# A two-layer graph network on one core: seven blocks split in rows 3 and 5, three masks and the low parts of x moved on VectorE

## The reference, cut to what matters

```python
# x: 4096 x 128, adj: 4096 x 4096 (nonnegative, mostly zero), all fp32
node = x @ W1                                   # 4096 x 16
hw   = einsum('nc,kcf->nkf', x, W2)             # 16 products of 128 x 128 weights
x0   = einsum('nk,nkf->nf', node, hw)
x1   = layernorm(x + relu(adj @ x0 + node @ b0))
msg  = x1 @ W + B
w    = where(adj < 1, exp(-(1/adj - 1)**2 * 2), 0)
out  = layernorm(x1 + w @ msg)
```

## Time and profile before

| what | value |
|---|---|
| median of 3 runs | 548.31 us (548.08 to 548.4) |
| the profiled execution, its own time | 548.46 us |
| its span | 546.6 us |
| PE busy | 541.2 us (99%), granted clock 1.0 throughout |
| DVE busy | 504.6 us (92%) |
| ACT busy | 498.2 us (91%) |
| POOL busy | 83.3 us (15%), all in stage one |
| DMA read | 139.62 MB |

### The profile page before, as it was taken

How to read it: one execution, slowest core, us unless ns; L and a number is a source line. 1 busy time by engine, 2 the same in 40 slices (tenths; PEclk the granted TensorE clock), 3 DMA queues, 4 the chain that set the end, 5 groups by cost and what they waited for, 6 DMA issues and landing times.

```text
span 546.6 us, 5236 instructions
## 1 busy us (share of the span) xinstructions
PE 541.2 (99%) x1800; PEld 332.0 (61%) x1800; DVE 504.6 (92%) x561; ACT 498.2 (91%) x449; POOL 83.3 (15%) x76
## 2 busy tenths in 40 slices
PE   9999999999999999999999999999999999999996
PEld 8888888655655565556555655565556556554444
DVE  5767777899999999999999999999999999999887
ACT  4778888669999999999999998999899899999994
POOL 1789989500000000000000000000000000000000
PEclk9999999999999999999999999999999999999999
DMA  5894000199998988888888898898988886870003
GB/s 165 321 424 173 27 2 0 31 367 422 414 360 300 339 335 315 303 330 314 334 306 314 321 349 305 312 317 320 327 315 308 316 330 236 322 267 1 0 19 135
DMA packets 23130, 142.05 MB, mean 260 GB/s; under 512 B 2720, under 2 KB 3264, under 8 KB 6720
## 3 DMA queue, kind: packets, MB, share of 16 engines
q1 hardware_dynamic: 22960, 141.46, 69.7%
q10 hardware_dynamic: 144, 0.26, 0.2%
HBM read 139.62 MB, written 2.10 MB: 259 GB/s over the span
## 4 chain that ended last, share of the span: by engine, by line
PE 99%; ACT 0%; DVE 0%; issue 0%; POOL 0%; ACTq 0%; POOLq 0%
PE kept_ps L526 20%; PE l_ps L526 18%; PE acc_ps L475 14%; PE acc_ps L464 7%; PE acc_ps L465 7%; PE acc_ps L466 7%; PE hw_ps L434 6%; PE hw_ps L440 5%; PE hw_ps L437 5%; PE acc_ps L526 2%; PE acc_ps L412 1%; PE var_ps L507 1%; PE acc_ps L481 1%; PE hw_ps L554 1%; PE acc_ps L536 0%; PE kept_ps L536 0%
## 5 line engine op out<-in xcount | busy, mean ns | idle before, releaser
L935 DVE SCALAR_TENSOR_TENSOR wt_pair<-wt_pair 128x2048 f32<-128x2048 f32 x60 | 136.9, 2283 | 1.3 <-DMA wt_pair<-adjT_dram 1.3
L642 ACT ACTIVATE wt_pair<-wt_pair 128x4096 f32<-128x4096 f32 (+1 forms) x33 | 108.9, 3300 | 11.7 <-DVE wt_pair L935 11.7
L647 ACT ACTIVATE wt_pair<-wt_pair 128x4096 f32<-128x4096 f32 (+1 forms) x33 | 109.1, 3307 | 0.5
L526 PE MATMUL kept_ps<-wt_pair,msg 128*128 128x512 f32 x240 | 107.9, 592 | 0.0
L923 DVE TENSOR_TENSOR row_lo<-rows,adj_hi 128x2048 fp32r<-128x2048 f32 x42 | 96.3, 2292 | 1.4
L526 PE MATMUL l_ps<-wt_pair,msg 128*128 128x512 f32 x216 | 97.1, 592 | 0.0
L626 ACT ACTIVATE prods<-hw_ps,node 128x128 f32<-128x128 f32 x256 | 73.1, 373 | 19.1 <-PE hw_ps L440 17.5
L890 DVE SCALAR_TENSOR_TENSOR part_acc<-hw_ps,node,part_acc 128x128 f32<-128x128 f32 x224 | 60.8, 343 | 20.7 <-PE hw_ps L440 20.7
L475 PE MATMUL acc_ps<-rows,x 128*128 128x512 f32 x176 | 78.8, 592 | 0.0
L464 PE MATMUL acc_ps<-adj_hi,x_hi 128*128 128x512 f32 x168 | 75.5, 449 | 0.0
L526 PEld LDWEIGHTS kept_ps<-wt_pair,msg 128*128 128x128 f32 x240 | 45.4, 190 | 49.3 <-issue 47.8
(11 more groups left out here) (122 smaller groups left out, 603.4 us busy)
## 6 DMA issues: line engine op xcount, KB each, us to landing
rows<-adjT_dram SPq DMA_DIRECT2D x68, 1024.0 KB, 4.9
wt_pair<-adjT_dram SPq DMA_DIRECT2D x60, 1024.0 KB, 4.8
x_in<-xT_dram SPq DMA_DIRECT2D x8, 256.0 KB, 3.6
x_row<-xT_dram SPq DMA_DIRECT2D x8, 256.0 KB, 5.1
outT_dram<-sumT SPq DMA_DIRECT2D x7, 256.0 KB, 2.0
W_in<-W_dram SPq DMA_DIRECT2D x3, 256.0 KB, 4.8
W_in<-W_dram ACTq DMA_DIRECT2D x1, 256.0 KB, 3.7
outT_dram<-sumT SPq DMA_DIRECT2D x2, 128.0 KB, 1.9
```

Of the source, the lines that this page charges most:

```text
L526: mm = pe.matmul(out, msg[:, c % 2, k, :], wt[t][:, k, :], start=(first and k == 0), stop=(last and k == CH - 1))
L642: act.activation(w, w, ACT.Ln, bias=TINY).then_inc(ln_made, 1)
L647: act.activation(w, w, ACT.Exp, scale=-1.0).then_inc(inv_made, 1)
L935: dve.scalar_tensor_tensor(out=w, in0=w, scalar=1.0, in1=w, op0=ALU.is_lt, op1=ALU.mult).then_inc(made, 1)
```

## The change

- The split blocks are a table by row. Rows 0, 2, 4 and 6 stay; row 1 gains block 6 (tile 14), row 3 block 2 (tile 26), row 5 block 2 (tile 42), row 7 block 6 (tile 62): 46 tiles are split.
- Block 2 of x0 needs high and low parts, one `round_x0` and one `remainder_of_x0` more. The low parts of blocks 1, 4 and 6 now overwrite x0 (with a wait for the last tile of that block that isn't split); only block 2 has memory of its own for its low part.
- The squares of pairs 28 and 44 go from DVE to ACT.
- Masks 0, 1 and 2 are done in stage one on DVE, after the sums of blocks 2, 4 and 6. For this SP loads the first six column tiles ahead of the first five row tiles.
- The low part of x of the next block is made on DVE, in the middle of `sum_over_k`, no longer on POOL.
- The written orders on DVE and ACT are changed all along stage two.

```diff
+SPLIT_IN_ROW = ((3, 5, 7), (1, 3, 5, 6, 7), (1, 3, 4, 5, 6, 7), (1, 2, 3, 4, 5, 6, 7), (1, 3, 4, 5, 6, 7), (1, 2, 3, 4, 5, 6, 7), (1, 3, 4, 5, 6, 7), (1, 3, 4, 5, 6, 7))
+LO_APART = tuple(g for g in SPLIT if any(g in row and g not in SPLIT_IN_ROW[-1] for row in SPLIT_IN_ROW))
+MORE_ON_ACT = (28, 44)
+MASKS_AFTER = (2, 4, 6)
...
-            return (m - FIRST_PAIR) % 4 >= 2 or m >= BY_TILE
+            return ((m - FIRST_PAIR) % 4 >= 2 and m not in MORE_ON_ACT) or m >= BY_TILE
...
+            for t in range(WT_RING - LATE_SLOTS):
+                load_wt(t)
             for i in range(ROW_RING):
                 load_row_tile(i)
-            for t in range(WT_RING - LATE_SLOTS):
-                load_wt(t)
...
                 for q in range(QUARTERS):
+                    if q == QUARTERS // 2 and g + 1 < NB:
+                        remainder_of_x(g + 1)
                     dve.wait_ge(hw_made[0], g * GROUPS + 2 * q + 2)
...
+                if g in MASKS_AFTER:
+                    mask(MASKS_AFTER.index(g))
...
             for g in range(NB):
-                if g + 1 < NB:
-                    remainder_of_x(g + 1)
                 fold(g)
```

More of the change, by code:

```diff
@@ L730, in _ @@
             take_ln(10)
+            square(1)
             take_inverse(10)
+            take_exp(8)
+            take_square(10)
+            take_ln(12)
             log_variance(1)
-            take_square(10)
+            take_inverse(12)
             inverse_root(1)
-            take_exp(8)
-            take_ln(12)
             take_exp(10)
-            take_inverse(12)
             take_ln(14)
+            take_exp(12)
             take_inverse(14)
-            take_exp(12)
             take_square(14)
@@ L910, in remainder_of_x0 @@
                 dve.wait_ge(x0_hi_made, n + 1)
+                if g not in LO_APART:
+                    at_least(dve, row_tile_done, max([i + 1 for i in range(g, TILES, NB) if not is_split(i)], default=0))
                 dve.tensor_tensor(x0_lo[g], x0[:, whole, :], x0_hi[:, mine, :],
@@ L1189, in _ @@
             mask(36)
+            split_row_tile(43)
             round_square(4)
+            take_square(32)
+            remainder_of_square(4)
             split_row_tile(44)
-            remainder_of_square(4)
-            take_square(32)
             mask(37)
+            split_row_tile(45)
+            scale_row(4)
             add_part(29)
+            split_row_tile(46)
             mask(38)
-            split_row_tile(45)
+            copy_messages(4)
+            add_part(31)
             mask(39)
-            scale_row(4)
-            split_row_tile(46)
-            add_part(31)
-            copy_messages(4)
-            mask(40)
             split_row_tile(47)
@@ L1254, in _ @@
             scale_row(6)
+            split_row_tile(62)
+            add_part(47)
+            copy_messages(6)
+            mask(56)
             split_row_tile(63)
-            copy_messages(6)
-            add_part(47)
-            mask(56)
             take_square(52)
@@ L1261, in _ @@
             take_square(54)
-            mask(58)
+            add_part(49)
             take_square(55)
@@ L1265, in _ @@
             mask(60)
+            mask(58)
+            mask(61)
             mask(59)
+            scale_row(7)
             take_square(56)
-            mask(61)
-            add_part(49)
             mask(62)
-            scale_row(7)
+            take_square(57)
+            copy_messages(7)
             add_part(51)
             add_row(7)
+            add_part(53)
+            take_square(58)
             mask(63)
-            copy_messages(7)
-            add_part(53)
-            take_square(57)
-            take_square(58)
             take_square(59)
             add_part(55)
-            take_square(60)
             add_part(56)
-            take_square(61)
             square2(0)
```

302 lines of the change are left out of this document (146 added, 156 removed).

## The result

| what | before | after |
|---|---|---|
| median of the runs | 548.19 us (4 runs, 545.88 to 548.4) | 560.11 us (4 runs, 557.66 to 562.55) |
| ratio, 95% interval | | **1.0237 (1.0202 to 1.0272)** |
| the profiled execution, its span | 548.46 us, 546.6 us | 562.55 us, 560.2 us |
| start of row tile 0 on PE | 103.15 us | 115.13 us |
| from there to the end of the span | 443.45 us | 445.07 us |

The change makes the kernel slower by 2.4% (the ratio of the table; the medians give 11.9 us, 2.2%, the two profiled spans 13.6 us). The forecast was 549.4, its range ended at 551.6. The last two rows show where it went: **12.0 us in stage one, 1.6 in stage two**, where +0.9 and +0.2 had been forecast.

What follows compares the result with a forecast made beforehand. The prediction took PE to set the time, with DVE and ACT nearly full. Its terms, -2.8 + 0.9 + 1.1 + 1.3 + 0.6 = +1.1 us, gave 549.56 for the profiled execution and 549.4 for the median, range 546.8 to 551.6.

Steps and rivals of the forecast that it cites:

- The subtraction itself: Stage one, low part of x on DVE: 0.60 us a block, hidden in DVE's 1.5 us wait, costing nothing.
- This is covered by 0.2; 0 to 0.5 each, and I take 0: Stage one, block ends: a 2.2 us mask delays the next eight sums, but PE was taken to lose nothing.
- rival 3: Stage one: DVE and POOL block each other when both read SBUF; 550.9 up to 556.0 us, chance 0.15.
- The dear end: Stage one: the fold goes first, each mask ends 2.4 us later, PE waits 2.2; three masks 6.6 us.
- x(4), +0.9: Stage one: load_x(3) goes 1.3 us later, so x(4) lands at 48.8 and PE waits 0.9 us.
- the three edges: Stage two: PE waits at column tile 0 (0.5 us), row tile 14 (0.6) and row tile 22 (1.3).
- the forecast's own bound: Row tile 22: if tile 12 lands after the median 4.8 us, its split is ready at 207.5 and PE doesn't wait.
- Later edges: Stage two from mask 12 to column tile 60: DVE's added load makes PE wait +0.6 us, bounds 0 and 1.0.
- -2.8: Stage two: four more split tiles take 2.8 us off PE, if PE waits for nothing new.
- Rival 1: Stage two: tiles 9 and 12 land quickly and both waits vanish; 547.0 us, chance 0.15.
- rival 2: No change: only tile 12 is quick, 548.1 us, or later edges hold and x(4) is absorbed, 547.9; chance 0.2.
- Rival 4: Stage two: DVE has become the bound and all 4.4 us behind mask 12 show; 553.2 us at most, chance 0.1.

Runs made afterwards that it cites:

- e5: The changed kernel with POOL's folds cut to one column in all but their last step; 550.65 us, one run.
- e8: The changed kernel with memsets, which only write, in place of all but the last step of POOL's folds; 550.76 us, one run.
- e10: The kernel before with the low part of x on DVE and x(4) loaded ahead of the last three 1 MB loads; 547.77 us, ratio 1.0031.
- e7: The changed kernel with low part on POOL, mask 9 behind the split of tile 14, split of tile 22 ahead of mask 16; 552.54 us.
- e11: The changed kernel with x(4) loaded ahead of the last three row tiles, nothing else; 560.82 us, ratio 1.0274.
- e3: The changed kernel with no mask in stage one, the low part of x still on DVE; 569.55 us, ratio 1.0433.
- e1: The changed kernel with stage one as before: low part on POOL, no masks there, old load order; 563.14 us, ratio 1.0293.
- e9: The kernel before with block 2 split in rows 3 and 5 and squares of pairs 28 and 44 on ACT; 559.96 us, ratio 1.0236.
- e2: The changed kernel with the low part of x back on POOL, the three masks staying in stage one; 553.21 us, ratio 1.012.
- e4: The kernel before with one edit, the low part of x made on DVE in the middle of the sums; 551.52 us, ratio 1.0079.
- e6: The changed kernel with POOL's second fold waiting for the mask in blocks with a mask; 556.85 us, ratio 1.0184.
- e12: The changed kernel with x(4) ahead, second fold behind the mask, mask 9 behind split 14, split 22 ahead of mask 16; 555.2 us, ratio 1.0161.

## Why the prediction was wrong

1. **The step that failed** is this: "The subtraction itself (0.60 a block) lies in DVE's wait for the third pair of groups (1.5 us a block) and costs nothing", and of the masks "This is covered by 0.2; 0 to 0.5 each, and I take 0". Both took durations from rows in which DVE had POOL at rest. They took 2.2 and 4.1 us. By e5 and e8, one run each, the exclusion with the half clock behind it makes 10.3 to 10.5 of the 12.4 us. At their own length the two terms would have been nearly right: in e5 the blocks other than that of x(4) lost nothing to a subtraction and 0.7 us in all to masks, and the totals, 550.65 and 550.76 us, lie inside the range. The forecast's own sign of rival 3, masks longer than 2.28 us in stage one, is the one that came.
2. The mechanism stood in the text, as rival 3, with 0.15, "mostly the cheap end". The trace of before couldn't show it, since there DVE did nothing with two SBUF inputs beside a fold, and I read silence as a small chance. The dear end was what happened: the folds came first, by 0.17 us at the first subtraction and 0.42 at mask 0. Its price, 6.6 at most, was too small by two terms: it priced the masks only, not the subtractions that gate load_x, and not the clock. Three waits of 1.6 to 2.4 us each brought a stretch at 1.2 GHz, 5.1 us together. A forecast that lets PE wait at all should price what the wait does to the clock.
3. x(4), +0.9: the chain was right link by link (subtraction, load_x(3), eleven 1 MB loads, x(4), ACT, PE), the size was not, because its first term was 0.68 instead of 2.79 us. With a subtraction of its own length block 3 still lost 1.4 (e5) and 1.2 us (e8), somewhat over 0.9. In after ACT waited 2.13, PE 1.65, and a half clock stretch followed. e10 confirms the chain by breaking it.
4. Stage two, the three edges: forecast 0.5 + 0.6 + 1.3 (its own figures, 209.9 less 208.5, give 1.4 for the last), measured 0.34 + 0.72 + 0.9, and the waits are gone in e7. Tile 9 did what was said: mask 9 began 44.80 us behind row tile 0, forecast 148.1 - 103.15 = 44.95. The wait at row tile 22 is in part luck. Tile 12 landed 4.8 us after its issue, not 7.4, so mask 12 waited 1.42 us instead of some 3 and began at 70.23, where 175.6 - 103.15 = 72.45 was forecast; by the forecast's own bound PE would then not have waited. But the way from mask 12 to the end of the split of tile 22 took 35.8 us instead of 34.2, because DVE stood 1.58 us before the split of tile 21 until PE had freed one of the two slots for high parts. The forecast had no such wait.
5. Later edges, forecast +0.6: stage two grew by 1.6 us to the end of the span and by 2.2 up to PE's last wait (matmul at 541.84 before, 556.07 after), and -2.8 + 0.34 + 0.72 + 0.9 leaves 2.4 to 3.1 of that for them. This is the second term that was far too small. e7's rows name the layernorm steps of the later rows as the main places. Which edit of the order makes which of these waits was not tried.
6. Rival 1 fell, since tile 9 came late. Half of rival 2 came true, tile 12 was quick, but the wait that this was to save came from the slot instead. Rival 4, DVE the bound, isn't borne out in its plain form: DVE is idle for 0.4 us in the window of row 3, before 0.2. But the later edges of item 5 are a milder case of it, and no run here tests that by itself.

What stays open: when a wait of PE brings the clock down. Its length alone doesn't tell: e11 has both outcomes at 1.59 us, and e3's of 1.77 left the clock up. Nor is it fixed for a kernel. The four runs of after have mean granted clocks of 0.989 to 0.996; the profiled one, with its three stretches, has 0.990, so by an estimate from that the fastest (557.66 us, 0.996) had one. On what it hangs no run here shows. Nor did I try the clock's part by itself; the 5.1 us are worked out from its level and the length of the stretches.

## What to carry to other kernels

Before moving work between VectorE and GpSimd, write beside each instruction how many of its inputs are in SBUF, and what the other engine reads at that moment: an instruction timed alone may take twice as long there, and who starts first decides on which side the loss lies. Then follow what the lengthened instruction releases, above all a buffer's load with a full queue behind it, down to the engine that sets the time. A hand-written order is one piece: taking half of it back (e1, e3) or half of it alone (e9) made stage two 12 to 18 us longer than before, so test such a change whole and mend it edge by edge.

## What the runs showed of the hardware

- The exclusion is settled by hundredths of a microsecond. The same mask takes 2.28 us when it comes 0.01 us before a fold (e2) and 4.13 when 0.42 after (after); a POOL that only writes never takes part (e8).
- A wait of PE of 1.6 to 2.9 us can cost more than itself: in after, e4, e6 and e11 the granted clock went to 0.50 from 0.1 to 2.3 us after PE had resumed, for 3.4 us or twice that; in e3, e11 and e12 waits of 1.2 to 1.8 us passed without it, and in three of e4's seven runs the mean clock leaves no room for such a stretch.
- A small load behind a full queue is late by the queue: 256 KB behind eleven loads of 1 MB landed 19.1 to 21.3 us after its issue, and 12.9 to 13.9 us when it stood ahead of the last three (e10 to e12).
- The first microseconds differ from run to run: in the profiled execution of before the clock rose only at 10.4 us (matmuls of 128x512 start every 0.43 us until then and every 0.23 behind it) and the node product of block 1 began at 13.83; after and e12 are alike (9.5 us); in the others it rose at 3.9 to 5.5 us and the product began at 11.1 to 11.6. The kernel before itself falls at about 548.3 or 545.8 us, 2.4 apart.
